# One head's maxima in two neighbouring PSUM banks, layer 0 of a four-layer block

## What is computed

```python
q = jnp.einsum('bte,fe->btf', query, Wq).reshape(Bsz, Tt, 2 * H, hd).transpose(0, 2, 1, 3)
k = jnp.einsum('bse,fe->bsf', query, Wk).reshape(Bsz, Tt, 2 * H, hd).transpose(0, 2, 1, 3)
...
scores = jnp.einsum('bhtd,bhsd->bhts', q, k)
attn_w = jax.nn.softmax(scores.astype(jnp.float32), axis=-1).astype(q.dtype)
...
aw = attn_w.reshape(Bsz, H, 2, Tt, Tt)
aw = aw[:, :, 0] - lam * aw[:, :, 1]
attn = jnp.einsum('bhts,bhsd->bhtd', aw, v)
```

## Time and profile before

| what | us |
|---|---|
| median of 3 runs (2055.1 to 2056.26) | 2056.09 |
| the profiled execution | 2057.91 |
| its span in the profile | 2056.1 |
| PE busy in the span | 1961.3 (95%) |
| DVE busy | 1551.9 (75%) |
| ACT busy | 1389.7 (68%) |
| POOL busy | 291.3 (14%) |
| layer 0's reduces, 512 of them (L1074, a0) | 585.9 |
| layer 1's reduces, 256 of them (L1074, a1) | 292.8 |

### The profile page before, as it was taken

How to read it: one execution, slowest core, us unless ns; L and a number is a source line. 1 busy time by engine, 2 the same in 40 slices (tenths; PEclk the granted TensorE clock), 3 DMA queues, 4 the chain that set the end, 5 groups by cost and what they waited for, 6 DMA issues and landing times. The chain is left out here.

```text
span 2056.1 us, 42997 instructions
## 1 busy us (share of the span) xinstructions
PE 1961.3 (95%) x16946; PEld 851.3 (41%) x16946; DVE 1551.9 (75%) x2254; ACT 1389.7 (68%) x2761; POOL 291.3 (14%) x534
## 2 busy tenths in 40 slices
PE   8999999999999989999988999999999899999998
PEld 4222222222223422222224666666675344444453
DVE  6999999999993589999936776777674655555553
ACT  4899999999997449999965776676673422222253
POOL 3122111222111341222200000000000200000000
PEclk7899999999999969999999999999999999999999
DMA  3001110110101020111010101110011155555510
GB/s 103 3 22 25 25 33 18 34 26 16 35 12 27 11 53 9 33 27 36 9 30 6 26 13 27 26 26 20 19 23 39 27 122 121 121 121 121 121 46 21
DMA packets 82632, 83.93 MB, mean 41 GB/s; under 512 B 29600, under 2 KB 64928, under 8 KB 78480
## 3 DMA queue, kind: packets, MB, share of 16 engines
q1 hardware_dynamic: 75344, 79.58, 16.2%
q0 software_dynamic: 6672, 1.23, 0.4%
q10 hardware_dynamic: 432, 0.56, 0.1%
HBM read 62.98 MB, written 2.42 MB: 32 GB/s over the span
## 5 line engine op out<-in xcount | busy, mean ns | idle before, releaser
L1074 DVE TENSOR_REDUCE a0nm<-ps 128x2 f32<-128x1024 f32 x512 | 585.9, 1224 | 3.0 <-PE ps L957 2.8
L1052 ACT ACTIVATE a0p<-ps 128x512 f32<-128x512 f32 x1024 | 546.6, 597 | 39.0 <-PE ps L966 17.2
L980 PE MATMUL ps<-a0p,a0vst 128*32 128x256 f32 x4096 | 328.3, 392 | 17.8 <-ACT a0p L1052 11.2
L966 PE MATMUL ps<-a0q,a0k 32*128 32x512 bf16 x1024 | 304.1, 387 | 0.0
L1074 DVE TENSOR_REDUCE a1nm<-ps 128x2 f32<-128x1024 f32 x256 | 292.8, 1218 | 9.0 <-PE ps L957 8.7
L1052 ACT ACTIVATE a1p<-ps 128x512 f32<-128x512 f32 x512 | 276.1, 596 | 26.3 <-PE ps L966 15.2
L2164 ACT ACTIVATE ex_s<-ps 128x512 f32<-128x512 f32 x128 | 76.4, 597 | 252.9 <-PE ps L2119 252.9
L957 PE MATMUL ps<-a0k,a0q 32*128 32x512 bf16 x1024 | 205.0, 398 | 9.2 <-DVE a0nm L1074 7.0
L966 PEld LDWEIGHTS ps<-a0q,a0k 32*128 32x128 bf16 x1024 | 86.4, 91 | 215.7 <-ACT a0p L1052 164.7
L2253 DVE TENSOR_TENSOR ex_su<-ex_s,ps 128x512 f32<-128x512 f32 x128 | 88.1, 688 | 114.6 <-PE ps L2123 114.0
L1764 PE MATMUL ps<-cak,caq 64*128 64x512 f32 (+3 forms) x768 | 171.1, 521 | 2.1 <-DVE canm L1916 2.1
(11 more groups left out here) (325 smaller groups left out, 2536.9 us busy)
## 6 DMA issues: line engine op xcount, KB each, us to landing
ex_wb<-ex_w_dram SPq DMA_DIRECT2D x62, 512.0 KB, 6.2
xc_res<-car_dram SPq DMA_DIRECT2D x32, 256.0 KB, 4.3
xc_res<-a0rec SPq DMA_DIRECT2D x15, 256.0 KB
a0q<-a0parts_sb SPq DMA_DIRECT2D x95, 32.0 KB, 2.0
a1q<-a1parts_sb SPq DMA_DIRECT2D x94, 32.0 KB
a0k<-a0parts_sb SPq DMA_DIRECT2D x90, 32.0 KB, 2.0
a1k<-a1parts_sb SPq DMA_DIRECT2D x84, 32.0 KB
a0q<-a0mr POOLq DMA_DIRECT2D x128, 4.0 KB, 1.6
```

What stands on the lines that cost most here:

```text
L966: pe.matmul(R.ps[:, score_bank(n), :], k[rows, place(u)[3], rt, s * 128:(s + 1) * 128], q[rows, place(u)[3], rt, place(u)[1] * CW:(place(u ...
L980: last = pe.matmul(R.ps[32 * j:32 * j + 32, 6, cols], vst[:, g, s, j * HG // 4, :], p[:, s % 2, j, cols], start=(g == 0 and s == 0 and hal ...
L1052: act.activation(p[:, s % 2, e, :], R.ps[:, score_bank(n), :], ACT.Exp).then_inc(exp_done, 1)
L1074: dve.tensor_reduce(nm[:, u % 2, 2 - 2 * z:4 - 2 * z, tb, hf], R.ps[:, bank:bank + 2, :], X_AXIS, ALU.max, negate=True).then_inc(bank_free, 1)
```

## The change

In layer 0 (`PAIRED`) alone, a slot now holds one head. Its two matmuls are the two halves of the keys of one head, in the two neighbouring banks, and DVE's reduce runs over all 1024 columns and writes one finished maximum straight into `m0`. `head_of` gives heads 0, 2, 1, 3 to slots 0 to 3 of each block of 128 queries, and the block is i // 4. `join` returns at once in layer 0; POOL's `split` waits for the last reduce of the unit itself (`bank_free`) and for the transpose before it (`mt_step`, now raised twice per unit instead of three times); `m0` has two buffers. The number of matmuls, their sizes and those of the reduces' input stay. In PE's stream no instruction changes its place: in each slot two matmuls of the same shape stand where two stood. What differs is the row group: before, the two of a slot lay on two groups (3 and 2, or 1 and 0), now both lie on the same one, 2 or 3 between scores 0 and 1, and 1 or 0 between scores 2 and 3.

```diff
--- before.py
+++ after.py
@@ -758,7 +758,7 @@
     rec = R.xc
     packed = sb("packed", [128, 2, 32])
     nm = sb("nm", [128, 2, 4, 4, 2])
-    m0 = sb("m0", [128, 4, 4])
+    m0 = sb("m0", [128, 2, 4, 4])
     m1 = sb("m1", [128, 4, 4])
     PAIRED = RT == 1
     mt = sb("mt", [128, 4, 4, 4] if PAIRED else [128, 4, 2, 4, 4], BF16)
@@ -789,6 +789,10 @@
     def slot_of(i):
 
         return i // 4, i // 2 % 2, (i + LEAD) % 2
+
+    def head_of(i):
+
+        return (0, 2, 1, 3)[i % 4]
 
     def ahead(u, s):
 
@@ -883,8 +887,13 @@
             shaped = (lambda x: x) if RT == 1 else (lambda x: x.rearrange("p (c d) t -> p c d t", d=2))
             part, none, done = (mt[:].rearrange("p h k t -> p k h t") if PAIRED else
                                mt[:, :, 0].rearrange("p t h k -> p t (h k)").rearrange("p t (d k c) -> p k c d t", d=2, c=2)), shaped(zero[:, 0:4, 0:4]), 4 + u * 3
-            lead, rest = shaped(m0[:]), shaped(m1[:])
-            pool.wait_ge(mt_step, 3 * u + 1)
+            lead, rest = shaped(m0[:, u % 2]), shaped(m1[:])
+            if PAIRED:
+                pool.wait_ge(bank_free, emptied("max", u, 15))
+                if u:
+                    pool.wait_ge(mt_step, 2 * u)
+            else:
+                pool.wait_ge(mt_step, 3 * u + 1)
             pool.tensor_tensor(part[:, 0], lead, none, ALU.add).then_inc(pool_step, 1)
             pool.wait_ge(pool_step, done + 1)
             pool.tensor_tensor(rest, lead, part[:, 0], ALU.subtract).then_inc(pool_step, 1)
@@ -895,7 +904,7 @@
         def maxima_rows(u):
 
             _k, chunk_i, _g, slot = place(u)
-            pool.wait_ge(mt_step, 3 * u + 3)
+            pool.wait_ge(mt_step, 2 * u + 2 if PAIRED else 3 * u + 3)
             for i in range(4):
                 if PAIRED:
                     to = q[A.spare_rows, slot, 0, chunk_i * CW:(chunk_i + 1) * CW].rearrange("p (v i t) -> p i v t", v=2, i=4)[:, i]
@@ -941,6 +950,7 @@
 
             kk, chunk_i, g, slot = place(u)
             tb, hf, z = slot_of(i)
+            tb = i // 4
             if i == 0 and chunk_i == 0:
                 by_pool = 0 if slot else A.n_pool_loads
                 pe.wait_ge(ld[slot], 16 * ((kk // 2 + 1) * A.n_loads + kk // 2 - by_pool))
@@ -952,6 +962,12 @@
                 queries = slice(first + 256 * (tb // 2) + tb % 2, first + 256 * (tb // 2) + 256, 2)
             else:
                 queries = slice(first + tb, first + CW, 4)
+            if PAIRED:
+                rows, rt = rows_of(head_of(i))
+                for hf in range(2):
+                    pe.matmul(R.ps[:, bank + hf, :], q[rows, slot, rt, queries],
+                              k[rows, slot, rt, hf * CW:(hf + 1) * CW], start=True, stop=True).then_inc(bank_full, 1)
+                return
             for d in (1, 0):
                 rows, rt = rows_of(2 - 2 * z + d)
                 pe.matmul(R.ps[:, bank + d, :], q[rows, slot, rt, queries],
@@ -1071,17 +1087,24 @@
             tb, hf, z = slot_of(i)
             dve.wait_ge(bank_full, filled("max", u, i))
             bank = dve_bank("max", u, i)
+            if PAIRED:
+                head = head_of(i)
+                dve.tensor_reduce(m0[:, u % 2, head, i // 4:i // 4 + 1], R.ps[:, bank:bank + 2, :].rearrange("p a t -> p (a t)"),
+                                  X_AXIS, ALU.max, negate=True).then_inc(bank_free, 1)
+                return
             dve.tensor_reduce(nm[:, u % 2, 2 - 2 * z:4 - 2 * z, tb, hf], R.ps[:, bank:bank + 2, :],
                               X_AXIS, ALU.max, negate=True).then_inc(bank_free, 1)
 
         def join(u):
 
+            if PAIRED:
+                return
             dve.wait_ge(bank_free, emptied("max", u, 15))
-            dve.tensor_tensor(m0[:], nm[:, u % 2, :, :, 0], nm[:, u % 2, :, :, 1], ALU.min).then_inc(mt_step, 1)
+            dve.tensor_tensor(m0[:, u % 2], nm[:, u % 2, :, :, 0], nm[:, u % 2, :, :, 1], ALU.min).then_inc(mt_step, 1)
 
         def turn(u):
 
-            dve.wait_ge(mt_step, 3 * u + 2)
+            dve.wait_ge(mt_step, 2 * u + 1 if PAIRED else 3 * u + 2)
             if u >= 2:
                 dve.wait_ge(rows_in, 64 * (u - 1))
             if PAIRED:
```

## The result

The changed kernel takes 2481.61 us (median of 4 runs, 2480.83 to 2482.3) where the one before took 2056.18 in the same comparison: 1.2074 times as long, 95% interval 1.2059 to 1.2089. I forecast 2064.7 us. The sign is right; the size is off by a factor of fifty.

A forecast was written before the change was run, and what follows sets the result against it. DVE's chain of reduces was taken to bound layer 0's loop, PE having 0.24 us reserve. Opening 5.1 + loop start 0.6 + steady loop 3.1 - 0.2 = +8.6 us on 2056.1 gave 2064.7 us; range 2057.5 to 2070.5.

The forecast's parts named there:

- The joins: DVE's chain in layer 0: dropping 32 joins of 0.08 us each gains 2.6 us if DVE stays the bound.
- The reduce's form: DVE's reduce in layer 0: one column out for 1024 instead of two costs 0, within +-0.005 us per reduce.
- POOL's split: POOL in layer 0: split starts about 1.2 us earlier, but nothing downstream moves, so 0.
- The pair on one row group: A slot's two matmuls on PE: each slot longer by 0.22 us at the upper clock, 0.43 at the lower.
- (a) The opening: Slots 2 to 14 of unit 0, clock 0.50: 3.0 us up to slot 8, then 2.1, together +5.1 us.
- (c) The steady loop: Layer 0's loop, upper clock: PE loses its reserve at takes, +0.21 us per two units, 15 takes, +3.1 us.
- (b) The start of the loop: Loop's first half steps: 1.55 becomes 1.98 us until the clock rises after two; +0.6 us, bounds 0 and 2.0.
- a clock that rises too early: Rival, chance 0.11: clock rises near slot 6, the opening hides its cost, about 2058.2 us.
- PE is the bound throughout: Rival, chance 0.09: a 0.09 us weight load adds to each pair, half step 1.21 us, about 2107 us.

The follow-up runs named there:

- e2: Changed kernel, but a slot's second matmul takes the neighbouring head, so the two lie on two row groups; 2051.83 us, ratio 0.9983 to the kernel before.
- e1: Changed kernel with 16 extra full-array matmuls on PE right before layer 0's first score; 2067.62 us, 1.0058 times the kernel before.
- e5: Changed kernel with one-head slots, without a join, from unit 2 on only, units 0 and 1 keeping two heads; 2058.41 us, ratio 1.0015 to the kernel before.
- e6: Changed kernel with one-head slots in units 0 and 1 only, two heads and joins from unit 2 on; 2065.02 us, ratio 1.0045 to the kernel before.
- e7: Changed kernel with 16 dense matmuls, behind a wait for ACT, ahead of unit 16's second pass; 2278.61 us, measured once.

## Why the prediction was wrong, point by point

- **The joins** (0.08 us each, 2.6 in all): right, 0.09 in e2. **The reduce's form, POOL's split**: 0, right.
- **The pair on one row group** (0.22 and 0.43 us later): right, 0.23 (e1) and 0.40 to 0.43.
- **(a) The opening**, +5.1 us: right, 5.2 from the first reduce to unit 0's transpose (29.81 us instead of 24.62). In the changed kernel's DVE timeline the reduces come 2.11 us apart to slot 8 and 1.48 to slot 14:

```profile
38.12 1.22 DVE L1092 TENSOR_REDUCE a0m<-ps 128x1 f32<-128x1024 f32 x1 [0.89 <-PE ps L968]
40.24 1.23 DVE L1092 TENSOR_REDUCE a0m<-ps 128x1 f32<-128x1024 f32 x1 [0.89 <-PE ps L968]
41.72 1.22 DVE L1092 TENSOR_REDUCE a0m<-ps 128x1 f32<-128x1024 f32 x1 [0.25 <-PE ps L968]
```

- **(c) The steady loop**, +0.21 us per two units: right for the clock that it assumed, 36.82 against 36.84 us (e1; 36.83 in e5). The lost reserve costs 0.37 us per pair, as I had it: e1's 36.82 less e2's 36.45.
- **(b) The start of the loop is the step that failed.** I wrote that each half step there "becomes 1.98" and then "with the clock rising after two of them". The first half is exact. The second I took from the kernel before, where the clock rose at 64.6 us, as if the time of the rise were given. It was the result of what PE did in just those half steps (e5, e6), and it was these that the change altered. With half steps of 1.98 instead of 1.13 us in 15 pairs of units and the lower clock before and behind them (403, 5 and 13 us), the terms (b) and (c), 3.5 us together, became some 421.
- **The rivals** held only a clock that rises too early. That it might not rise at all was missing, though the text had both numbers for its price: 480 x (1.98 - 1.13) = 408 us. "PE is the bound throughout" was there, at 2107 us, but for a weight load that can't hide. That load does hide: the Trainium skill's sentence ("TensorE: Matmul & The Clock Gate", Part 3, The mechanism) that a weight load overlaps only matmuls of another row group is not what e1 shows, where two matmuls with the same stationary operand on one group start 0.23 us apart, no 0.09 more, and the second's load lies within the first's time. The way out that the same section names, the background weight buffer, fits.

What stays open: which property of PE's work in a half step the clock answers to. The same number of matmuls is done in 1.55 us with two heads per slot and in 1.98 with one, PE is busy throughout in both, and the first lifts the clock. The changed kernel's own last unit says a little more. Its second pass has no slots, its half steps take 1.55 us too (scores at 1029.77 and 1031.32), and the clock does not rise:

```profile
1029.00:1064.00 35.00, 35.00 (x230) 6.82 (x222) 4.72 (x17) 25.00 (x48) 7.93 (x12) 0.50 0.16 40
```

So neither a busy PE nor a half step of 1.55 us is enough by itself. I tried nothing that separates the longer half step from the missing overlap of the pair, or the shared row group from the shared stationary operand.

## What to carry to other kernels

When a stretch runs at PE's lower clock before it rises, treat the rise as a result, not as a date: ask for each edit in that stretch whether it would still come, and price the case that it does not over all the work behind it. Read the granted clock as well as the busy share, because a PE that is busy all the time can be at half speed for a long time, here for 984 us. Small matmuls that run side by side on different row groups are worth keeping so where the clock has still to rise, even if the time of the pair seems hidden behind another engine: at the upper clock the overlap was worth 0.37 us per two units, at the lower it decided over 425 us in all.

## What was not expected of the hardware

- In the changed kernel the lower clock held for 984 us with PE busy for 979. In e7 the same loop left it after 500 us, within a block of dense matmuls of some 4 us, and in e1 a block of 5.6 us ahead of the loop kept the loop out of it.
- PE's records start out of program order across row groups, but the results are signalled in program order. In the half step at 401.50 us above, the program has slot, slot, score; the score's record (401.51, L982) starts 0.40 us ahead of that of the slot's second matmul (401.91, L968), which waits for its rows. The semaphore updates in the same trace tell of the ends: 402.12 us for the first score, 402.15 and 402.55 for the two of the slot, and 402.58 for the second score, 0.03 behind the slot's second. The same 0.03 us stand in 463 half steps from 80 to 1000 us. So nobody could use that score before the slot's second matmul was done; what it did in between, the trace does not say.
